# Second chunk's in-projection in the scan's PSUM banks, 5 to 8 slots sooner in the orders

## What is computed

```python
resid_norm = resid * rsqrt(mean(resid * resid) + EPS) * norm_w
x_in = resid_norm @ W_in                       # the in-projection, 512 -> 1024
x = silu(conv(x_in, 4 taps) + conv_b)          # depthwise, along the sequence
delta = softplus(x @ W_delta_1 @ W_delta_2 + b_delta_2)
Bm = x @ W_B
Cm = x @ W_C
# scan over the sequence, for each of 1024 channels and 16 states
h = h * exp(delta * A) + (delta * x) * B_l
y = sum over states of h * C_l
```

## Time and profile before

| | before |
|---|---|
| median of three runs | 2184.05 us (2183.57 to 2187.59) |
| the profiled execution's own time | 2178.91 us |
| its span (first to last instruction) | 2177.1 us |
| busy share: PE, DVE, ACT, POOL | 87%, 79%, 79%, 85% |
| mean granted TensorE clock | 0.961 of full |
| DMA over the span | 425.92 MB, mean 196 GB/s |
| first scan instruction begins at | 113.18 us |

### The profile page before, as it was taken

The page is one execution under the profiler, slowest core; times in us unless marked ns, Lnnn a source line. Parts: engine busy times, 40 slices in busy tenths (PEclk is TensorE's granted clock), DMA queues, the critical chain, the costliest instruction groups (busy, mean ns, idle before and its releaser), DMA issues.

```text
span 2177.1 us, 35466 instructions
## 1 busy us (share of the span) xinstructions
PE 1893.4 (87%) x12005; PEld 1585.3 (73%) x12005; DVE 1726.6 (79%) x2529; ACT 1716.2 (79%) x3404; POOL 1859.3 (85%) x1256
## 2 busy tenths in 40 slices
PE   5677777999999998999999898999989898989883
PEld 4566767878787786878778786978778686767551
DVE  3487878898898989888888988888898978888332
ACT  3489797979888897979889897988889798888221
POOL 1299999899999999999999999999989899999312
PEclk9999898999999999999999999999999999999995
DMA  5656566765766575765756585765757464645310
GB/s 174 209 189 212 184 212 206 241 215 190 242 201 223 170 265 175 245 220 184 253 177 228 186 269 177 226 227 183 250 162 250 149 229 166 218 151 184 116 49 20
DMA packets 234672, 425.92 MB, mean 196 GB/s; under 512 B 18623, under 2 KB 134907, under 8 KB 234491
## 3 DMA queue, kind: packets, MB, share of 16 engines
q1 hardware_dynamic: 234490, 423.65, 59.0%
HBM read 339.18 MB, written 84.41 MB: 195 GB/s over the span
## 4 chain that ended last, share of the span: by engine, by line
PE 31%; POOL 16%; DVE 15%; ACT 10%; issue 7%; DMA 7%; DVEq 0%; SPq 0%; POOLq 0%; ACTq 0%
DVE h L971 10%; POOL hc L613 9%; PE mixed L1363 6%; PE bank L1152 6%; PE y_sum L1157 6%; PE pair_bank L1283 4%; DMA c_all<-bc_dram 4%; ACT u_t L747 3%; PE routed L1337 3%; POOL operand L597 2%; DVE hv L1034 2%; ACT operand L728 2%; DMA dx_q<-dx_dram 2%; PE routed L1237 1%; DMA dx_dram<-dx 1%
## 5 line engine op out<-in xcount | busy, mean ns | idle before, releaser
L613 POOL TENSOR_TENSOR hc<-h,c_all 128x1024 f32<-128x1024 f32 x512 | 1205.0, 2367 | 83.0 <-DVE h L971 76.0
L971 DVE TENSOR_TENSOR_SCAN h<-operand,carry,bank 128x512 f32<-128x512 f32 x528 | 649.2, 1266 | 126.1 <-PE bank L1152 112.7
L747 ACT ACTIVATE u_t<-dx_t,lbc 128x256 f32<-128x256 f32 x1408 | 631.8, 498 | 19.0 <-PE bank L1152 18.9
L1157 PE MATMUL y_sum<-ident,hc 128*128 128x128 f32 x4096 | 601.6, 278 | 7.5 <-POOL hc L613 6.8
L1152 PE MATMUL bank<-ident,u_t 128*128 128x128 f32 x2816 | 448.6, 284 | 165.5 <-DVE h L971 162.6
L1152 PEld LDWEIGHTS bank<-ident,u_t 128*128 128x128 f32 x2816 | 336.3, 145 | 274.1 <-issue 176.3
L1157 PEld LDWEIGHTS y_sum<-ident,hc 128*128 128x128 f32 x4096 | 490.7, 144 | 47.1 <-issue 27.5
L728 ACT ACTIVATE operand<-delta_q,neg_a 128x512 f32<-128x512 f32 x704 | 480.0, 711 | 0.0
L597 POOL TENSOR_TENSOR operand<-dx_q,b_all 128x1024 f32<-128x1024 f32 x160 | 378.4, 2365 | 8.4 <-DMA b_all<-bc_dram 8.4
L728 ACT ACTIVATE bank<-delta_q,neg_a 128x512 f32<-128x512 f32 x320 | 218.1, 682 | 204.1 <-DVE h L971 203.7
L971 DVE TENSOR_TENSOR_SCAN h<-bank,carry,operand 128x512 f32<-128x512 f32 x240 | 295.8, 1268 | 27.4 <-POOL operand L597 17.0
(11 more groups left out here) (119 smaller groups left out, 1858.5 us busy)
## 6 DMA issues: line engine op xcount, KB each, us to landing
c_all<-bc_dram SPq DMA_DIRECT2D x256, 512.0 KB, 4.3
b_all<-bc_dram SPq DMA_DIRECT2D x160, 256.0 KB, 5.5
win<-in_L_attn_W_in SPq DMA_DIRECT2D x64, 512.0 KB, 6.0
wskip<-in_L_attn_W_skip SPq DMA_DIRECT2D x64, 512.0 KB, 6.5
x_dram<-x SPq DMA_DIRECT2D x64, 256.0 KB, 6.2
delta_dram<-delta SPq DMA_DIRECT2D x32, 512.0 KB, 7.6
dx_dram<-dx SPq DMA_DIRECT2D x32, 512.0 KB, 5.3
delta_q<-delta_dram SPq DMA_DIRECT2D x32, 512.0 KB, 5.9
```

Of the source, the lines that this page charges most:

```text
L613: nc.gpsimd.tensor_tensor(hc[:, number % 3], h[:, number % 3], c_all[:, j % 2, s % 2:s % 2 + 1].to_broadcast([P, 2, SPAN]), ALU.mult).then ...
L747: last = nc.scalar.activation(u_t[:, j % 2, b], dx_t[:, k, b], ACT.Copy, scale=lbc[:, stage % 2, b, DELTA + n:DELTA + n + 1])
L971: nc.vector.tensor_tensor_scan(h[:, number % 3, q], first, second, start, ALU.mult, ALU.add).then_inc(scan_done.sem, 1)
L1157: return matmul(to, lhsT=of, rhs=ident[:], is_transpose=True, start=start, stop=stop, skip_group_check=True)
```

## The change

Let SECOND be step 2, the step whose prep is that of chunk 1. For that prep alone, the slots are `TAPPED_SECOND = (-12, -7, -2, 4)` in place of `(-5, 1, 6, 10)`. Its in-projection goes to the scan's banks, `bank[:, p % 2]`, and so do its tanh and what reads them. PE's wait for the delta_ready of the chunk before falls away for it, and ACT's exponential into `bank` gets a wait for the last x_ready of step 2, which takes effect once. With the slots move, in their engines' orders: PE's in-projection; ACT's last tap and tanh; DVE's taps and x; and SP's four stores of x. `load_win` and everything else keep their slots, as do all other chunks.

```diff
+TAPPED_SECOND = (-12, -7, -2, 4)
+SECOND = -1 - FIRST
+def tapped(t, p):
+    return (TAPPED_SECOND if t == SECOND else TAPPED)[p]
+        def in_bank(t, p):
+            return bank[:, p % 2] if t == SECOND else pair_bank(p)
...
                                 for p in range(PAIRS):
-                                    if s == TAPPED[p] + 6:
+                                    if s == tapped(t, p) + 6:
                                         if v := due(sp, x_ready, t, p + 1):
                                             sp.wait_ge(x_ready.sem, v)
...
                         if v := due(act, scan_done, t, 2 * (s - 1) + q + 1):
                             act.wait_ge(scan_done.sem, v)
+                        if v := due(act, x_ready, SECOND, PAIRS):
+                            act.wait_ge(x_ready.sem, v)
                         to = bank[:, q]
...
-                                    if s == TAPPED[p] + 4:
+                                    if s == tapped(t, p) + 4:
...
-                                        nc.scalar.activation(pair_bank(p)[:],
+                                        nc.scalar.activation(in_bank(t, p)[:],
...
-                                    if s in (TAPPED[p], TAPPED[p] + 2):
-                                        e = (s - TAPPED[p]) // 2
+                                    if s in (tapped(t, p), tapped(t, p) + 2):
+                                        e = (s - tapped(t, p)) // 2
...
-                                if (s, late) in ((TAPPED[p] - 3, 1), (TAPPED[p] - 2, 0)):
-                                    e = s - TAPPED[p] + 3
-                                    if not p and (v := due(pe, delta_ready, t - 1, PAIRS)):
+                                if (s, late) in ((tapped(t, p) - 3, 1), (tapped(t, p) - 2, 0)):
+                                    e = s - tapped(t, p) + 3
+                                    if not p and t != SECOND and (v := due(pe, delta_ready, t - 1, PAIRS)):
                                         pe.wait_ge(delta_ready.sem, v)
...
-                                        last = matmul(pair_bank(p)[:, e * T:(e + 1) * T],
+                                        last = matmul(in_bank(t, p)[:, e * T:(e + 1) * T],
```

More of the change, by code:

```diff
@@ L819, in _ @@
                                 for p in range(PAIRS):
-                                    if s == TAPPED[p]:
+                                    if s == tapped(t, p):
                                         if v := due(act, in_done, t, 2 * p + 2):
@@ L827, in _ @@
                                             last = scaled(hv[:, p % 2, e, TAPS - 1:],
-                                                          pair_bank(p)[:, e * T + TAPS - 1:(e + 1) * T],
+                                                          in_bank(t, p)[:, e * T + TAPS - 1:(e + 1) * T],
                                                           taps[:, et, TAPS - 1:TAPS], cbias[:, et:et + 1])
@@ L1018, in _ @@
                                             out=x[:, 2 * p:2 * p + 2, :].rearrange("p e t -> p (e t)"),
-                                            in0=pair_bank(p)[:], scalar=1.0,
+                                            in0=in_bank(t, p)[:], scalar=1.0,
                                             in1=hv[:, p % 2].rearrange("p e t -> p (e t)"), op0=ALU.add,
@@ L1022, in _ @@
                                 for p in range(PAIRS):
-                                    if s in (TAPPED[p], TAPPED[p] + 2):
-                                        e = (s - TAPPED[p]) // 2
+                                    if s in (tapped(t, p), tapped(t, p) + 2):
+                                        e = (s - tapped(t, p)) // 2
                                         et = 2 * p + e
                                         row, halo = hv[:, p % 2, e], edge[:, et]
-                                        got = pair_bank(p)[:, e * T:(e + 1) * T]
+                                        got = in_bank(t, p)[:, e * T:(e + 1) * T]
                                         if v := due(dve, xin_ready, t, p + 1):
@@ L1042, in _ @@
                                         if e:
-                                            pair = pair_bank(p).rearrange("p (e t) -> p e t", e=2)
+                                            pair = in_bank(t, p).rearrange("p (e t) -> p e t", e=2)
                                             copied(tail[:, 2 * p:2 * p + 2], pair[:, :, T - width:]).then_inc(
```

## The result

| | before | changed |
|---|---|---|
| median, 19 runs each | 2183.71 us (2179.94 to 2187.59) | 2190.1 us (2182.66 to 2196.03) |
| ratio of the two | | 1.0025, 95% interval 1.0015 to 1.0035 |
| the profiled execution's own time | 2178.91 us | 2188.29 us |
| first scan starts at | 113.18 us | 116.31 us |

The changed kernel is slower by 0.25%, 5.5 us by that ratio (the two medians lie 6.4 us apart). The interval, 3.3 to 7.6 us, shuts out that nothing changed, and the 0.2% line (4.4 us) that the chances were cut at lies inside it. The forecast was +3.0 us, 2187.0, with 2181.5 to 2191.5 as its range. The start-up went as the forecast had it, nearly row by row. By this pair of profiles, what it missed lies behind the first scan. The slots of the four pairs moved by 7, 8, 8 and 6, so by 6 to 8 and not by 5 to 8.

The account below looks back on a forecast made before the run. The start-up chain ahead of the first scan was taken to bound the effect: pair 1's 2.2 us lead becomes 2.9 us lost at pair 2, +3.0 at the lbc copy; 2184.05 + 3.0 = 2187.0 us, range 2181.5 to 2191.5.

Parts of the forecast that it names:

- What bounds the kernel: Start-up before the first scan: one chain across engines, none full; a microsecond on it delays everything after by a microsecond.
- Rival (d): The change doesn't do what it says, or the 160 us behind the first scan shift a few us either way; chance 0.06.
- likeliest case: The forecast's own case for the whole kernel: slower by 1 to 4.4 us; chance 0.58.
- Part 1: Chunk 1's pair 0 brought forward on PE: chunk 0's delta 3.96 us later, x of pair 0 2.5 us sooner.
- Part 2: Chunk 1's pair 1, in-projection behind the last delta product: x at 73.4 against 75.56, 2.2 us of lead left.
- Part 3: SP's queue: pair 2's weights wait behind stores, so its last tap is 2.9 us later than now.
- clock term: Pair 2's in-projection on PE after idling: 1.6 us lost to the low granted clock, bounds 0 and 2.0.
- Part 4: From pair 3 to the first scan: lbc copy at 92.3, +3.0 us, scan at 116.2; added ACT wait and banks cost nothing.
- The table load: ScalarE's table load in the start-up: 1.28 us without the skill page's added drain; by the page 0.7 us more.
- (a): Break-even: pair 2's load lands in 4.2 us or less and PE keeps its clock, 2184.0 to 2185; chance 0.12.
- (b): Slower by more: landing 5.4, whole pair 2 at low clock, lbc copy 94.1, +4.7, 2188.8 us; chance 0.20.
- (c): Lead kept: pair 2's weights in place by 68.9, x of pair 3 at 83.6, time 2180.5 us; chance 0.04.

Follow-up runs that it names:

- bare delay: The kernel before with only two more copies on ACT ahead of the second chunk's copy of low, lengthening the start-up; ratio 1.0025 (1.0014 to 1.0036).
- both loads first: The changed kernel with pair 2's and pair 3's weight loads for the second chunk issued ahead of the stores of x; ratio 0.998 against the kernel before.
- thirteen matmuls: The changed kernel with 13 more 128x256 matmuls on PE between pair 1's and pair 2's in-projection of the second chunk; ratio 1.0008 against the kernel before.
- stores back: The changed kernel with only SP's four stores of x for the second chunk back at their old slots; ratio 1.0028 against the kernel before.
- only the banks: The changed kernel with the old slots for the second chunk, so banks changed and PE's delta wait gone; ratio 0.9995 against the kernel before.
- pair 0 later: The changed kernel with both loads first and slots (-10, -6, -2, 4), pair 0 behind the first delta products; ratio 0.9988 against the kernel before.

## Why the prediction was right or wrong

- **What bounds the kernel, and that the whole effect is the shift of the first scan.** Right in kind: the time has the sign of the first scan's shift in all nine kernels, and a bare delay gives the changed kernel's ratio. Short in size: 3.0 us were forecast, and 5.5 were timed (3.3 to 7.6). The step that fell short is "after the first scan nothing in the program changes, so I take the whole effect to be the shift of that scan". What a start-up of another length meets behind the first scan was put at nothing. In the changed kernel's first profile the first 32 scans took 57.5 us, and in four others whose first scan stands from 114.5 to 117.1, one of them without any of the change, 56.8 to 57.3; against the 55.3 us of the second profile of before that is 1.5 to 2.2 us more. 3.1 and 2.2 make 5.3. In the changed kernel's second profile it was the start-up, 4.5 us against the second profile of before, and 0.2 us behind it. Both come near 5.5, by different ways; what the share of each is over the timed runs isn't known. The other 2.4 us of the 7.7 at the 33rd scan are luck of before's first profile, which had the full clock from 125 to 170. They were in my reading of the result and not in the sum: that took from the profile only rows ahead of the first scan, which agree in both (113.18 and 112.99), and started from the median of the runs. Rival (d) named such an effect, with a chance of 0.06; it was a part of the likeliest case.
- **Part 1.** Right: pair 0 from 54.59 (54.95 forecast), softplus 60.57 (60.9), x of pair 0 over at 67.67 (67.95), held by dx. Of the 0.3 us by which these are sooner than forecast, 0.2 are the start of the stretch, which is that much sooner in this execution; pair 0 also starts 0.2 us ahead of the end of the turning, where I had it start behind it.
- **Part 2.** Right: x of pair 1 over at 72.88 (73.4).
- **Part 3.** Right, and shown by "both loads first": issue at 68.66 (68.85), landing in 5.0 us between the bounds of 4.2 and 5.4, PE on at 73.70 (73.65), last tap at 79.47 (79.05). The clock term was 1.6 us, and it measured 2.0 by the run with thirteen matmuls, 0.4 us that stand in the last tap. The upper bound was the better value. That is also what the rule of the Trainium skill on DMA waits between matmuls would have given ("TensorE: Matmul & The Clock Gate", "Loop structure matters more than you think"), and the granted clock of 0.50 from 71 to 77 us agrees with it. The name of the cause was too narrow, as "stores back" shows: the stores of x are one part, the late store of dx ahead of them and the traffic of two loads at once are others, and taking one away brings out another.
- **Part 4.** Right: lbc copy at 92.39 (92.3), first scan at 116.31 (116.2); no cost of the added wait on ACT and of the banks shows ("only the banks").
- **The table load.** Right as read: in the changed kernel too it is 1.28 us and the next activation follows at once, at 60.57 behind 59.28 + 1.28 and at 65.65 behind 64.35 + 1.28. The 0.7 us that the prediction works out for a longer one counts only the second of these two loads, though both stand ahead of x of pair 0; as neither is longer, nothing hangs on it.
- **The rivals.** (a), that load and clock are kind, didn't come. (b) named the low clock over the whole pair, +3.8 us at the last tap and the lbc copy at 94.1: in the changed kernel's second profile they were +4.4 (80.58) and 93.76, with the clock at 0.50 from 70 until about 80. So (b)'s start-up comes too, in one of two profiles. Its time, 2188.8, is nearer to the 2190.1 measured than the forecast's, but the execution in which its start-up was seen took 2185.97. I had given (b) 0.20, and slower by over 0.2% 0.24. With (b)'s start-up in one of two profiles and the ratio just above that line, both were low. (c), the lead kept, didn't come with this change. It can be had: with both loads first the first scan is at 109.43, and 4.4 us are won, where (c) said 3.6.

## What to carry over

When a step is moved in a hand-written order, list the other queues in which its inputs and outputs stand: here PE, ACT, DVE and the stores moved and two loads of weights didn't, and a lead of 2.8 us became a delay of 3.1. Put the loads where their buffers come free, one by one; two that came out of the queue together took 7.0 and 7.5 us, and the one needed first had nothing from its place. A gap read between two profiled executions has the luck of both in it: at the 33rd scan it was 7.7 us in one pair and 4.7 in another, at the last 9.9 and 1.0. So profile both kernels a second time before explaining a difference of that size.

## What the runs showed that I had not expected

- Useless matmuls in a wait pay: 5.8 us of them, ahead of a load that lands no sooner, brought the last tap 3.75 us behind PE's start in place of 5.77, and made the kernel 3.7 us faster. 3.6 us of them in the same wait left the clock to fall at 74.3, and nothing gained showed in the time.
- An idle time of 2.4 to 2.7 us on PE can go either way. The clock stayed at 1.0 behind 2.66 us at 70.6 in the first profile of before, and in the second, of the same program, it was at 0.50 from 72 on behind 2.66 us at 70.7. In "pair 0 later" it was at 0.50 behind 2.39 us at 67.9, and in "only the banks" behind 2.66 us at 69.5.
- Two loads of 512 KB issued 0.9 us apart behind a store of 512 KB, with one of 256 KB issued 1.4 us behind them, took 7.0 and 7.5 us. The same two loads issued 3.5 us apart took 4.2 and 3.6 us in the kernel before.
- Which way the first 32 scans went shows in one number: 56.8 to 57.5 us in the five profiles with a granted clock of 0.77 from 140 to 155 us, 52.9 to 55.5 in the seven with 0.84 or more.
